# Expert tiles instead of dense products for half of the feed-forward chunks

## What is computed

```
x = x + 0.5 * ffn(layernorm(x));  x = x + attn(layernorm(x));  x = x + 0.5 * ffn(layernorm(x))
ffn:  scores = sigmoid(x @ gate_w.T); sc = scores + gate_bias        # 64 experts in 8 groups of 8
      keep the 4 groups with the largest sum of their two best sc; tidx = top 8 of sc in these
      tw = scores[tidx] / (sum + 1e-20) * 2.5                        # other experts: weight 0
      for each expert e: y += w[:, e] * ((silu(x @ We_gate[e]) * (x @ We_up[e])) @ We_down[e])
      y += (silu(x @ Ws_gate) * (x @ Ws_up)) @ Ws_down               # shared expert, every token
```

## Time and profile before

| | us |
|---|---|
| runs, median (lowest to highest) | 1830.77 (1829.75 to 1831.84) |
| profiled execution, its own time | 1831.43 |
| its span | 1829.7 |
| TensorE, VectorE, ScalarE, GpSimd busy | 1781.7, 1331.9, 774.6, 36.6 |
| packets on the one DMA queue | 109488, 149.08 MB, 36.9% of 16 engines |

### The profile page before, as it was taken

How to read it: one execution, slowest core, us unless ns; L and a number is a source line. 1 busy time by engine, 2 the same in 40 slices (tenths; PEclk the granted TensorE clock), 3 DMA queues, 4 the chain that set the end, 5 groups by cost and what they waited for, 6 DMA issues and landing times.

```text
span 1829.7 us, 30208 instructions
## 1 busy us (share of the span) xinstructions
PE 1781.7 (97%) x9049; PEld 1255.0 (69%) x9049; DVE 1331.9 (73%) x3327; ACT 774.6 (42%) x1971; POOL 36.6 (2%) x84
## 2 busy tenths in 40 slices
PE   5899999999999999999999999879999999999999
PEld 3566666666666667777778777756666666666665
DVE  5777677676776678888888888767677676777765
ACT  3333323233232256767666666633323233232322
POOL 0000000000000000000000000000000000000000
PEclk8999999999999999999999999999999999999999
DMA  9954554455545500000000000034554455544553
GB/s 206 173 122 110 115 117 105 107 115 115 117 100 109 116 1 2 0 0 0 0 0 0 0 0 0 1 82 109 120 118 108 107 122 121 117 104 111 120 124 75
DMA packets 109530, 149.60 MB, mean 82 GB/s; under 512 B 30128, under 2 KB 43056, under 8 KB 109488
## 3 DMA queue, kind: packets, MB, share of 16 engines
q1 hardware_dynamic: 109488, 149.08, 36.9%
HBM read 144.87 MB, written 4.19 MB: 81 GB/s over the span
## 4 chain that ended last, share of the span: by engine, by line
PE 61%; DVE 2%; DMA 0%; issue 0%; ACT 0%; SPq 0%; POOLq 0%; POOL 0%; DVEq 0%
PE banks L521 12%; PE banks L489 7%; PE banks L487 7%; PE banks L488 7%; PE banks L1059 6%; PE banks L1099 5%; PE banks L1080 4%; PE banks L1116 3%; PE banks L1024 2%; PE banks L1063 2%; PE banks L1025 2%; PE banks L1026 2%; PE banks L1043 1%; PE banks L1044 1%; PE banks L1042 1%; DMA f_mix_wide<-mix_rows 0%
## 5 line engine op out<-in xcount | busy, mean ns | idle before, releaser
L592 ACT ACTIVATE f_hid<-banks 128x512 f32<-128x512 f32 x528 | 315.4, 597 | 835.9 <-PE banks L521 831.5
L648 DVE TENSOR_TENSOR f_hid<-banks,f_hid 128x512 f32<-128x512 f32 x528 | 363.9, 690 | 338.0 <-ACT f_hid L592 336.3
L521 PE MATMUL banks<-f_hid,wd 128*128 128x512 f32 x1056 | 540.7, 594 | 10.7 <-DVE f_hid L659 10.6
L487 PE MATMUL banks<-r_xT_hi,wg_hi 128*128 (+1 forms) x528 | 393.0, 744 | 2.4 <-PEq L951 2.4
L659 DVE TENSOR_TENSOR f_hid<-f_mix_wide,f_hid 128x512 f32<-128x512 f32 x512 | 352.9, 690 | 38.4 <-DMA f_mix_wide<-mix_rows 24.3
L521 PEld LDWEIGHTS banks<-f_hid,wd 128*128 128x128 f32 x1056 | 196.8, 188 | 67.6 <-DVE f_hid L659 13.1
L487 PE MATMUL banks<-r_xT_hi,wu_hi 128*128 (+1 forms) x528 | 209.9, 398 | 0.0
L489 PE MATMUL banks<-r_xT_lo,wu_hi 128*128 (+1 forms) x528 | 209.9, 398 | 0.0
L488 PE MATMUL banks<-r_xT_hi,wu_lo 128*128 (+1 forms) x528 | 208.8, 396 | 0.0
L489 PE MATMUL banks<-r_xT_lo,wg_hi 128*128 (+1 forms) x528 | 208.3, 394 | 0.0
L488 PE MATMUL banks<-r_xT_hi,wg_lo 128*128 (+1 forms) x528 | 207.3, 393 | 0.0
(11 more groups left out here) (153 smaller groups left out, 2155.4 us busy)
## 6 DMA issues: line engine op xcount, KB each, us to landing
f_mix_wide<-mix_rows SPq DMA_DIRECT2D x252, 512.0 KB, 6.5
landing<-in_L_ffn_We_gate SPq DMA_DIRECT2D x4, 512.0 KB, 7.1
landing<-in_L_ffn_We_up SPq DMA_DIRECT2D x4, 512.0 KB, 7.8
wd<-in_L_ffn_We_down SPq DMA_DIRECT2D x4, 512.0 KB, 6.8
mix_rows<-r_mixT SPq DMA_DIRECT2D x32, 64.0 KB, 2.1
out<-x_all SPq DMA_DIRECT2D x8, 256.0 KB, 6.7
f_mix_wide<-mix_rows SPq DMA_DIRECT2D x4, 384.0 KB, 5.4
f_mix_wide<-mix_rows SPq DMA_DIRECT2D x4, 128.0 KB, 3.0
```

Source lines behind the costliest of these rows:

```text
L487: nc.tensor.matmul(bank[:, :], hi, rhs_hi, start=start, stop=False)
L521: nc.tensor.matmul(acc[:, :], w["wd"][:, p * P:(p + 1) * P], hid[:, p % HIDS, :], start=(p == 0), stop=(p == PAIRS)).then_inc(down_done, 1)
L592: nc.scalar.activation(hid[:, p % HIDS, :], gate_bank[p % 3][:, :], ACT.Silu).then_inc(silu_done, 1)
L648: nc.vector.tensor_tensor(hid[:, p % HIDS, :], up_bank[p % 3][:, :], hid[:, p % HIDS, :], ALU.mult)\
```

## The change

The new kernel computes 4 of 8 chunks of each feed-forward densely, and for the other 4 it sends each token's row to the 8 experts chosen for it.

- **Dense chunks**: as before, but gate, up and down are plain fp32 matmuls on unsplit weights, three a slot. Feed-forward one has chunks 0 to 3 dense (132 slots, then the quads); two has chunk 4, then the quads, then chunks 5 to 7. Routing takes three steps a slot.
- **Routing of sparse chunks** keeps a mask of chosen experts; TensorE counts tokens per expert and ranks them; VectorE works out the first row of each expert (`plan`), row numbers (`place`) and weights (`weigh`).
- **Dispatch**: GpSimd scatters each tile of normed rows to x_rows in DRAM, 8 times, one indirect DMA of 128 rows (64 KB) each: 128 in a feed-forward. x_rows is cleared to zero first, in twelve 1 MB transfers issued by ScalarE.
- **Quads**: SP loads 4 tiles of rows (256 KB); TensorE transposes them, multiplies by gate and up of each tile's expert (whose number it loads into registers), turns hid, multiplies by down; VectorE copies the result and SP stores it to y_rows. 48 quads, and 4 before them for the shared expert of the sparse chunks, from SBUF.
- **Combine**: GpSimd gathers each token's 8 results (128 indirect DMAs), VectorE adds each with its weight. For feed-forward one this lies inside attention, half a tile (4 gathers, 4 adds) a step; for two inside the last three dense chunks, one tile in five slots.
- **Attention** is written out without a loop. The copies of q and v are ScalarE's. The fronts (norm, logits) and routing of the sparse chunks of feed-forward two and of its first dense chunk run inside it; GpSimd scatters from step 49 on, the rest after it.

The core of the diff (the route steps up to 17 are as before):

```diff
+SPARSE = 4
+DENSE = 4
+TILES = (TOPK * SPARSE * CHUNK - E) // P + E
+QUADS_R = -(-TILES // CT)
+ROWS = QUADS_R * CHUNK
+QUADS_ALL = SPARSE + QUADS_R
+PAD = E // 2
+YBUFS, STORE_LAG, GBUFS = 3, 6, 3
+HALVES = (range(0, TOPK // 2), range(TOPK // 2, TOPK))
...
+FIRST = routes_of([(0, True), (1, True), (4, False), (5, False), (6, False), (7, False), (2, True), (3, True)])
+SECOND = routes_of([(0, False), (1, False), (2, False), (3, False), (4, True), (5, True), (6, True), (7, True)],
+                   by_row=SPARSE + 1)
...
+        def dispatch(i):
+            tile, half = divmod(i, 2)
+            k, t = divmod(tile, CT)
+            if t == 0 and half == 0:
+                pool.wait_ge(idx_done, k + 1)
+            for j in HALVES[half]:
+                nc.gpsimd.indirect_dma_start(
+                    x_rows[:, :], bass.IndirectOffsetOnAxis(ap=b.idx[:, f, CT * k + t, j:j + 1], axis=0),
+                    b.xk[:, k, t, :], None).then_inc(scattered, 16)
...
+        def gather(t, js=range(TOPK)):
+            if t >= GBUFS and js[0] == 0:
+                pool.wait_ge(added, added_before + TOPK * (t - GBUFS + 1))
+            for j in js:
+                nc.gpsimd.indirect_dma_start(
+                    g_buf[:, t % GBUFS, j, :], None, y_rows[:, :],
+                    bass.IndirectOffsetOnAxis(ap=b.idx[:, f, t, j:j + 1], axis=0)).then_inc(gathered[t % GBUFS], 16)
...
+        def add(t, js, chunk_of):
+            x = x_all[:, chunk_of[t // CT] * CT + t % CT, :]
+            for j in js:
+                if j == 0:
+                    dve.wait_ge(gathered[t % GBUFS], 16 * TOPK * (times_before[t % GBUFS] + t // GBUFS + 1))
+                    if t % CT == 0:
+                        dve.wait_ge(r.weigh_step, WEIGH_STEPS * (t // CT + 1))
+                else:
+                    dve.wait_ge(added, added_before + TOPK * t + j)
+                nc.vector.scalar_tensor_tensor(x, g_buf[:, t % GBUFS, j, :], b.w8[:, f, t, j:j + 1], x,
+                                               ALU.mult, ALU.add).then_inc(added, 1)
...
+        def load_experts(j):
+            if j < SPARSE:
+                expert[j] = [E] * CT
+                return
+            i = j - SPARSE
+            if i == 0:
+                pe.wait_ge(r.plan_step, PLAN_STEPS - 1)
+            _, expert[j] = nc.values_load_multi_w_load_instructions(
+                b.ids[i:i + 1, :], engines=PE_ONLY, min_val=0, max_val=E,
+                skip_runtime_bounds_check_because="the number of 64 experts that end at or before a tile")
+
+        def gate_up(j):
+            load_experts(j)
+            e = expert[j]
+            pe.wait_ge(xT_copied, j + 1)
+            if j >= 2:
+                pe.wait_ge(hid_done, j - 1)
+            for t in range(CT):
+                wt = w["gu"][:, :, e[t], :] if j < SPARSE else \
+                    w["gu"][:, :, bass.ds(e[t], 1), :].rearrange("p k a f -> p k (a f)")
+                mm = nc.tensor.matmul(B[j % 2][:, t * P:(t + 1) * P], q.xqT[:, j % 2, t * P:(t + 1) * P], wt,
+                                      start=True, stop=True)
+            mm.then_inc(gu_done, 1)
...
+        def step(j):
+            if ok(j):
+                turn(j)
+            if ok(j - 1):
+                gate_up(j - 1)
+            if ok(j - 2):
+                turn_hid(j - 2)
+            if ok(j - 3):
+                down(j - 3)
...
+        def load(i):
+            if i == 0:
+                sp.wait_ge(r.scattered, 16 * TOPK * CT * SPARSE)
+            if i >= 3:
+                sp.wait_ge(turned, SPARSE + i - 2)
+            sp.dma_start(q.xq[:, i % 3, :, :], rows(x_rows, i)).then_inc(loaded[i % 3], 16)
+
+        def store(i):
+            sp.wait_ge(y_read, SPARSE + i + 1)
+            sp.dma_start(rows(y_rows, i), q.yq[:, i % YBUFS, :, :]).then_inc(y_stored[i % YBUFS], 16)
+
+        def step(i):
+            if i < QUADS_R:
+                load(i)
+            if i >= STORE_LAG:
+                store(i - STORE_LAG)
+
...
+            rows = F if p == PAIRS else P
+            experts = slice(2 * p, 2 * p + rows // F)
+            if g >= 3:
+                pe.wait_ge(silu_done, g - 2)
+            if ready and c == 0:
+                ready(pe, p)
+            nc.tensor.matmul(gate_bank[g % 3][0:rows, :], w["gu"][:, 0, experts, :].rearrange("p e f -> p (e f)"), x,
+                             start=True, stop=True).then_inc(gate_done, 1)
+            if g >= 3:
+                pe.wait_ge(gated, g - 2)
+            nc.tensor.matmul(up_bank[g % 3][0:rows, :], w["gu"][:, 1, experts, :].rearrange("p e f -> p (e f)"), x,
+                             start=True, stop=True).then_inc(up_done, 1)
...
+            for k in range(STEPS):
+                pool.wait_ge(scores_done, 2 * k + 1)
+                if k < 2 * SPARSE * CT:
+                    gather(k // 2, HALVES[k % 2])
+                if k >= A_DISPATCH:
+                    dispatch(k - A_DISPATCH)
+                if front_row(k, 6) is not None:
+                    front_rstd(front_row(k, 6))
+                if moments_row(k) is not None:
+                    rstd_of(moments_row(k))
...
+FIRST_AT = {1: 3, 2: 12, 3: 20, 4: 28, 5: 36, 6: 47, 7: 76}
+COUNT_AT, PLAN_AT, PLACE_AT, PLACE_GAP, WEIGH_AT = 50, 51, 56, 5, 62
+SCATTER_AT = [58 + (5 * i) // 2 for i in range(2 * SPARSE * CT)]
+CLEAR_AT = tuple(range(16, 52, 3))
...
+SECOND_AT = {5: 3, 7: 2 * SLOTS + 1}
+Q_AT = 6
+C_FROM, C_GAP = SLOTS + 6, 5
+STORE_AFTER = {(1, 7): 0, (2, 4): 1, (3, 1): 2, (3, 6): 3}
...
+                if i == dispatched + 3:
+                    rstd_of(in_dense[0])
+                dispatch(i)
+            rstd_of(among)
+            for side in range(YBUFS):
+                pool.wait_ge(qd.y_stored[side], 16 * len(range(side, QUADS_R, YBUFS)))
+            last = -(-(SECOND_AT[7] - C_FROM) // C_GAP) + 1
+            for t in range(SPARSE * CT):
+                if t == last:
+                    rstd_of(in_dense[1])
+                gather(t)
```

More of the change, by code:

```diff
@@ new lines, with routes_of @@
+ROWS = QUADS_R * CHUNK
[3 more added lines that the diff above has]
+HALVES = (range(0, TOPK // 2), range(TOPK // 2, TOPK))
+DENSE_STEPS = 25
+SPARSE_STEPS = 23
+PLAN_STEPS = 12
+PLACE_STEPS = 4
+W_STEPS = 3
+WEIGH_STEPS = W_STEPS * CT + 5
+@dataclass(frozen=True)
+class Route:
+    n: int
+    front: int
+    chunk: int
+    dense: int
+    sparse: int
+def routes_of(kinds, by_row=0):
+    out, d, s = [], 0, 0
+    for n, (chunk, is_dense) in enumerate(kinds):
+        out.append(Route(n, n - by_row, chunk, d if is_dense else -1, -1 if is_dense else s))
+        d, s = d + is_dense, s + (not is_dense)
+    return out
@@ new lines, in rank, with copy_xT, sigmoid, copy_mixT @@
+        def rank(k):
+            take_misc(rank_read, k + 1)
+            nc.tensor.matmul(misc[:, 0:CT * E], w["before"][:, :], b.mask[:, k, :], start=True, stop=False)
+            nc.tensor.matmul(misc[:, 0:CT * E], w["ones"][:, :], b.run[:, k, :], start=False, stop=True)\
+                .then_inc(rank_done, 1)
+        return turn_xn, logits, turn_mix, count, rank
+    def on_scalar(act, misc):
+        def copy_xT(r, free=None):
+            act.wait_ge(xn_turned, r.front + 1)
+            if r.dense >= 2:
+                act.wait_ge(*free)
+            elif r.sparse >= 1:
+                act.wait_ge(logits_done, r.front)
+            nc.scalar.copy(xT_of(r), misc[:, :]).then_inc(xT_done, 1)
+        def sigmoid(r):
+            act.wait_ge(logits_done, r.front + 1)
+            if r.dense >= 1:
+                before = max(q.n for q in order[:r.n] if q.dense >= 0)
+                act.wait_ge(route_step, steps_before(order, before + 1))
+            nc.scalar.activation(score_of(r), misc[:, 0:CT * E], ACT.Sigmoid).then_inc(score_done, 1)
+        def copy_mixT(r):
+            act.wait_ge(mix_turned, r.dense + 1)
+            if r.dense >= 1:
+                act.wait_ge(mix_stored, 32 * r.dense)
+            nc.scalar.copy(me.d.mixT[:, :], misc[:, 0:CHUNK // 2]).then_inc(mixT_done, 1)
+        return copy_xT, sigmoid, copy_mixT
@@ L931, in row_norm, with attention @@
     return parts
-def attention(nc, w, x_all, banks, psum, rows, ahead):
+A_ROUTE, A_COUNT, A_PLAN, A_RANK, A_DISPATCH = 14, 44, 45, 48, 49
+A_HEAD, A_MIX = 47, 55
+ADD_LAG = 3
+def attention(nc, w, x_all, banks, psum, rows, b, mix_rows, y_rows, first, second, gathered, added):
     TB = SEQ // P
@@ L942, in attention @@
     QUADS = H // 4
-    STEPS = 2 * QUADS
+    STEPS = NB * QUADS
+    PER_CHUNK = CHUNK // SEQ
+    FRONTS = [4 * n for n in range(SPARSE * PER_CHUNK)] + [32, 37]
+    chunk_of = [q.chunk for q in FIRST if q.sparse >= 0]
+    later, head = [q for q in SECOND if q.sparse >= 0], SECOND[SPARSE]
     NPB = P + SEQ
@@ L1111, in output @@
                         pe.wait_ge(x_updated, b)
-                    if not (last and k == QUADS):
+                    if b + 1 < NB:
                         pe.wait_ge(xT_lo_done, b + 2)
@@ L1159, in slot @@
```

(4 more changed lines are left out.)

1800 lines of the change are left out of this document (1134 added, 666 removed).

## The result

| | before | changed |
|---|---|---|
| runs, median (lowest to highest), us | 1831.3 (1829.8 to 1833.2) | 1977.98 (1971.99 to 1979.97) |
| ratio to before, 95% interval | 1 | 1.0795 [1.077, 1.082] |
| span of the profiled execution, us | 1829.7 | 1976.5 |
| mean granted TensorE clock | 0.994 | 0.932 |

The change makes the kernel 8% slower where 4.9% faster was forecast, outside the range. That number can't be read without another one: the same kernel, unchanged, took 1721.61 us on a second chip (1716.95 to 1723.78, ratio 0.9398 [0.9377, 0.9419]), inside the range, while the kernel before has a median of 1830 to 1833 us on every chip.

What follows compares the result with a forecast made beforehand. TensorE was taken to bound both feed-forwards and attention, DMA the start. 414 + 177 + 604 + 95 + 177 + 265 + 8 = 1740 span, 1741 against the median, 4.9% less; range 1630 to 1860.

Steps and rivals of the forecast that it cites:

- Row transfers: GpSimd's 128 scatters and 128 gathers in each feed-forward: 1.5 us each, between 1.0 and 2.6, all hidden.
- The rival for it: Row transfers starved or slow: others wait for late transfers; decides from 1.94 us each, 2007 us at 2.4; chance 0.12.
- The rule of the Trainium skill: Attention's normalisations on VectorE could lock out GpSimd's descriptors, DMA 620 to 3100 ns; sum kept at 1741 by the rows.
- Dense slots and quads: Feed-forwards: three fp32 matmuls make a dense slot 2.60 us against 2.25; a quad takes 3.3 us, 52 of them 177.
- The term of 0.85 us for four register loads: Quads: loading four expert numbers into TensorE's registers adds 0.85 us a quad, taken between 0.4 and 2.6.
- the rival of dear quads: TensorE's queue sets the quads, as register loads block it: 5.0 us a quad, total 1917; decides from 4.17; chance 0.16.
- Feed-forward one, dense: Its four dense chunks before the quads end at 414 us: 128 + 261 + 7 + 13 + 5.
- The 13 us for routing: Feed-forward one's dense slots: VectorE's 2.84 us against TensorE's 2.60 costs 10 over 42 slots, the last route 3.
- The fronts: Feed-forward one, dense part: seven more fronts put a transposition and logits on TensorE, about 1 us each, 7 in all.
- Attention: 559 us before plus 45 (between 15 and 90) for v's copy, late second maxima, and fronts, ranks and counts: 604.
- ScalarE's copy of v: Attention: v's copy comes last in ScalarE's order and TensorE waits for it, about 0.2 us x 64 = 13.
- Feed-forward two: First dense chunk 95 us, quads 177, three last chunks with fronts 265, tail and store 8.

Runs made afterwards that it cites:

- the spaced kernel: The changed kernel with feed-forward transfers each waiting for its own slot and attention's sent two and two; 1724 us, or 1742 with three marking runs where increments were held.
- half_rows: The changed kernel with each of the 512 indirect transfers moving 64 rows instead of 128; 1999.73 us, ratio 1.0923.
- mixed_second: The changed kernel without gathers, dummy transfers in attention's steps 4 to 43, real scatters spaced from step 56 and in feed-forward two; 1856.63 us, one run.
- direct: The changed kernel with each of the 512 indirect transfers made a plain one of 128 consecutive rows; 1710.88 us, ratio 0.9328.
- paced: The changed kernel with GpSimd waiting for dense slots' progress before every second transfer, and attention's meant to go two per half step; 1825.88 us, ratio 0.9966.
- placed_marked2: The spaced kernel plus three runs of four dummy indirect transfers in attention's steps 37 to 39, second try; 1742.38 us, ratio 0.952.
- placed: The changed kernel with each feed-forward transfer waiting for its own slot, attention's two behind first scores and two behind second bias; 1723.94 us, ratio 0.9423.
- after_again: The changed kernel unchanged, run again as a control on the second chip; 1721.61 us, ratio 0.9398.
- mixed: The changed kernel without gathers, with dummy indirect and plain transfers in attention's steps 4 to 43, real scatters four a step from 49; 1717.95 us, one run.

## Why the prediction was wrong, point by point

- **Row transfers: the step that failed.** "At 1.5 all are hidden." They are shorter than forecast, 0.96 us and 1.26 from start to start, and hardly late for anyone: in the changed kernel SP's first row load didn't wait for a scatter, and VectorE waited for a gather once, 1.7 us, so the waits that were to show the forecast wrong didn't come. Their term in the sum was 0, and on the chip of the result it was 258 us, with TensorE's increments coming late beside them, by 9.9 us in the timeline above. I priced an engine off the path by its own cover and asked only who waits for its results. Nothing in the trace of before could show that its transfers delay another engine's signals, but the range of an operation with no row there should have had an end for a cost to others, not only for its own length.
- **The rival for it** (decides at 1.94 us a transfer) had the right actor and the wrong mechanism: at 1.26 us its prices are all zero. That it names a time of 2007, close to 1978, is luck; its chance of 0.12 was for something else. Its 9.1 us a step also doesn't fit the forecast's own 604 / 64 = 9.4, which moves the 2007 by 11 at most.
- **The rule of the Trainium skill** (SBUF — State Buffer, SBUF: two separate sides), that a two-port fp32 operation of VectorE keeps GpSimd from writing descriptors, didn't show (that the normalisations are such operations is taken from their rate alone). Beside the normalisations of attention a gather took 0.95 us in the median, as elsewhere; the changed kernel, second chip, scatters and gathers:

```profile
L467 POOL DMA_INDIRECT x_rows<-r_xk,r_idx x256: 953/962/1487, 225.3 to 1293.1; - x128
...
L501 POOL DMA_INDIRECT a_g<-y_rows,r_idx x128: 940/954/1190, 582.8 to 895.9; - x128
```

- **Dense slots and quads.** Three downs of steady slots (2.58 us apart, forecast 2.60) and three first transpositions of quads (2.78 apart, forecast 3.3), same kernel and chip, answering:

```profile
321.14 1.02 PE L794 MATMUL banks<-f_hid,wd 128*128 128x512 f32 x2
...
323.72 1.02 PE L794 MATMUL banks<-f_hid,wd 128*128 128x512 f32 x2
...
326.29 1.02 PE L794 MATMUL banks<-f_hid,wd 128*128 128x512 f32 x2
...
501.64 0.66 PE L556 MATMUL banks<-ident,f1q_xq 128*128 128x128 f32 x4
...
504.43 0.66 PE L556 MATMUL banks<-ident,f1q_xq 128*128 128x128 f32 x4
...
507.21 0.66 PE L556 MATMUL banks<-ident,f1q_xq 128*128 128x128 f32 x4
```

  The slot was right. The term of 0.85 us for four register loads was too large by 0.5, 28 us in the first feed-forward and 31 in the second; the rival of dear quads (over 4.17) is excluded.
- **Feed-forward one, dense**: 428 against 414 where nothing is held. Slot 33 came at 134 instead of 128. The 13 us for routing didn't arise, as slots with three routing steps take 2.58. The fronts were mis-sized instead, 7 us for seven: slots 38 to 41 and 49 to 52 alone took 19 us more than eight slots, and TensorE's transpositions (L165) wait for the norm, 20 us in the whole kernel. Waits of TensorE, same kernel and chip (line waited for: us in total, times, longest):

```profile
PE banks L1163 <- DVE a_oT L1448: 48.9, 31, 3.3
PE banks L165 <- DVE f_xn L254: 12.6, 6, 5.2
...
PE banks L165 <- DVE r_xk L254: 7.9, 3, 3.9
```

- **Attention**: 626 against 604, inside 574 to 649, and 627 without any transfer. Steps without routing and additions stayed at 8.35 to 8.6, so ScalarE's copy of v cost next to nothing of its 13. What was 22 too few seems to lie in steps in which VectorE is late with the copy of o (the first line above); how much of it is routing and how much additions wasn't parted.
- **Feed-forward two**: 96.4 and 272.2 against 95 and 273. Right.
- Together 1718.6 against 1740, the errors being +14, -28, +22, +1, -31 and -1, rounded. The sum came within 21 us where its missing term is zero, in part by luck, as 38 us too little stood against 59 too much. The chance of 0.77 for faster was too high because all cases shared one assumption, that hidden work is free.

## What to carry to other kernels

An engine that starts a new kind of work can slow the others without being waited for. When engines idle together and their waits are put down to "remote" or "issue", compare the end of the producer with the update of its semaphore before looking for a busy resource. Keep indirect transfers of GpSimd apart (two at a time, and at a point of the step where no increment of TensorE is urgent): it cost 2 us where it wasn't needed, no more than the spread of the runs, and where it was the spaced kernel took some 235 less than the changed one on another chip. Run the kernel unchanged beside every set of experiments, on the same chip, or give each experiment its own control.

## What the runs showed of the hardware

- On some chips indirect DMAs of GpSimd, four or more in a row, hold back TensorE's semaphore increments: by up to 2.5 us in a group of four, one let through about every 5 us in a long run (half_rows). Three in a row hold some by up to 1.1, two real scatters and two by up to 0.7, one or two dummies by 0.2 at most (mixed_second). Plain DMAs from GpSimd's queue don't (direct, mixed_second), and the increments of VectorE and ScalarE that are recorded are at most 0.4 late. The chips of the result, of paced, of mixed_second and of placed_marked2 did it, those of placed, of after_again and of mixed didn't; the last came twice and was the same both times. The kernel before has no such transfers and took 1829 to 1835 us on all.
- 64 rows a transfer cost no less than 128, and take 0.89 us of GpSimd instead of 0.96. A plain one takes 0.54.
- The two kinds of chip can be told by one number of the trace: where increments are late, only 27 to 52% of the landings of GpSimd's transfers have a record (changed: 2376 of 8192, sixteen a transfer), elsewhere 99 to 100% (changed, second chip: 8127).
- Left open: why only some chips, by what path the increments are held, whether it is the chip or the way the program lay on it, and whether the recording of a trace, which loses its records in just these runs, has a part in the delay. The chip of the result isn't known to be another than one of the three that showed it later.
